# The first sample's mixed weight is spread over the quadrants by TensorE, and the first layer 0 moves up behind the mixtures

## The reference

```
x = x + (sum_k att0[b,k] W0[k]) @ x + att0 @ bias0        # conditional 1x1 layer
x = x + grouped_conv(x, 9 taps, 4 groups) + c_weight @ cond + fside
x = x + (sum_k att2[b,k] W2[k]) @ x + att2 @ bias2
x = x + (sum_k att3[b,k] W3[k]) @ x + att3 @ bias3
att_n = softmax(gelu(gelu(cond W0 + b0) W1 + b1) W2 + b2)   # K = 8 options
```

## Time and profile before

| | |
|---|---|
| median of 3 runs | 484.31 us (484.07 to 484.46) |
| the profiled execution | 484.36 us |
| its span, first to last instruction | 482.5 us |
| TensorE busy, of the span | 476.7 us (99%) |
| VectorE, ScalarE, GpSimd busy | 321.0, 249.0, 152.3 us |
| granted TensorE clock, mean | 1.00 |

### The profile page before, as it was taken

The page is one execution under the profiler, slowest core; times in us unless marked ns, Lnnn a source line. Parts: engine busy times, 40 slices in busy tenths (PEclk is TensorE's granted clock), DMA queues, the critical chain, the costliest instruction groups (busy, mean ns, idle before and its releaser), DMA issues.

```text
span 482.5 us, 17714 instructions
## 1 busy us (share of the span) xinstructions
PE 476.7 (99%) x8003; PEld 472.3 (98%) x8003; DVE 321.0 (67%) x409; ACT 249.0 (52%) x414; POOL 152.3 (32%) x151
## 2 busy tenths in 40 slices
PE   8999999999999999999999999999999999999996
PEld 8988999999999999999999999999999999999996
DVE  2648697767676876766687776767777676777424
ACT  3664455466444545654455466444545654455544
POOL 2935172324243222413331331434233142320110
PEclk9999999999999999999999999999999999999999
DMA  8696977676546477664657667464767746452224
GB/s 283 205 332 161 306 243 224 215 221 210 186 119 211 155 221 219 205 220 114 201 151 215 214 215 217 125 210 134 215 206 220 219 150 206 130 188 78 90 88 175
DMA packets 39243, 92.86 MB, mean 192 GB/s; under 512 B 4600, under 2 KB 25472, under 8 KB 35200
## 3 DMA queue, kind: packets, MB, share of 16 engines
q1 hardware_dynamic: 39168, 91.73, 61.2%
HBM read 53.95 MB, written 37.77 MB: 190 GB/s over the span
## 4 chain that ended last, share of the span: by engine, by line
PE 98%; DMA 0%; DVE 0%; issue 0%; DVEq 0%
PE cv_ps L499 56%; PE aux_ps L479 18%; PE aux_ps L528 17%; PE cv_ps L435 2%; PE cv_ps L422 1%; PE aux_ps L422 1%; PE cv_ps L528 1%; DMA m_rep<-in_net_dram 0%; PE aux_ps L457 0%; PE cv_ps L401 0%; PE aux_ps L376 0%; PE cv_ps L376 0%; DVE y_all L838 0%; PE aux_ps L391 0%; PE aux_ps L446 0%
## 5 line engine op out<-in xcount | busy, mean ns | idle before, releaser
L499 PE MATMUL cv_ps<-x_hi,conv_lo 32*128 32x512 f32 x1536 | 322.5, 391 | 0.0
L499 PE MATMUL cv_ps<-x_hi,conv_hi 32*128 32x512 f32 x1536 | 322.2, 389 | 0.0
L499 PE MATMUL cv_ps<-x_lo,conv_hi 32*128 32x512 f32 x1536 | 322.0, 391 | 0.0
L499 PEld LDWEIGHTS cv_ps<-x_hi,conv_lo 32*128 32x128 f32 x1536 | 202.6, 183 | 0.4
L499 PEld LDWEIGHTS cv_ps<-x_hi,conv_hi 32*128 32x128 f32 x1536 | 202.5, 183 | 0.4
L499 PEld LDWEIGHTS cv_ps<-x_lo,conv_hi 32*128 32x128 f32 x1536 | 202.4, 184 | 0.3
L770 DVE SCALAR_TENSOR_TENSOR x_lo<-cv_ps,d_all,x_hi 128x512 fp32r<-128x512 f32 x128 | 87.2, 743 | 131.0 <-ACT x_hi L617 131.0
L627 ACT ACTIVATE y_all<-aux_ps,e_all 128x512 f32<-128x512 f32 x122 | 74.0, 690 | 134.1 <-PE aux_ps L528 134.1
L479 PE MATMUL aux_ps<-x_hi,a_hi 32*128 32x512 f32 x512 | 115.5, 391 | 0.3 <-issue 0.3
L479 PE MATMUL aux_ps<-x_lo,a_hi 32*128 32x512 f32 x512 | 114.8, 388 | 0.0
L479 PE MATMUL aux_ps<-x_hi,a_lo 32*128 32x512 f32 x512 | 114.8, 388 | 0.0
(11 more groups left out here) (104 smaller groups left out, 512.4 us busy)
## 6 DMA issues: line engine op xcount, KB each, us to landing
x_sb<-in_x_dram SPq DMA_DIRECT2D x31, 1024.0 KB, 6.5
out_dram<-y_all SPq DMA_DIRECT2D x60, 512.0 KB, 7.4
a_rep<-a_pairs SPq DMA_DIRECT2D x64, 128.0 KB, 7.2
m_rep<-m_pairs SPq DMA_DIRECT2D x64, 128.0 KB, 6.3
out_dram<-y_all SPq DMA_DIRECT2D x8, 256.0 KB, 2.6
a_pairs<-a_all SPq DMA_DIRECT2D x1, 1920.0 KB, 11.3
m_pairs<-m_all SPq DMA_DIRECT2D x1, 1792.0 KB, 11.8
m_all<-in_mix_dram SPq DMA_DIRECT2D x2, 512.0 KB, 5.3
```

What stands on the lines that cost most here:

```text
L499: mm = pe.matmul(cv_ps[:, g, :], w[rows(g), j, :], a[n % 2][rows(g), q, s:s + T], start=(i == 0), stop=(i == steps - 1))
```

## The change

- The weight of sample 0 no longer goes through DRAM to its first use. Behind mixture 12+c quadrant c multiplies its 32 rows of `a0_all` by a 32 by 128 block of identities, which puts them on all 128 partitions of bank c of `cv_ps`. ScalarE makes the high part of the four results, VectorE the low part (`a0_first_hi`, `a0_split`). `split_a0(0)` of GpSimd goes.
- These four banks are slots 16 to 19 of the ring of 7, so mixture t has slot t up to 15 and slot t+4 from there on. The order of the banks in the ring is another one, and so is `BY_SCALAR`: 14 of 24 copies on ScalarE as before.
- Layer 0 of sample 0 follows in each quadrant directly behind its last mixture. Then comes the whole of the last bias, then all eight groups of pair products, then the steady part.
- The first biases stand behind turn 15 and not 11. The empty places of the first three turns take six idle matmuls.
- SP issues the load of the second x ahead of its first wait, and that of the third x ahead of the large save of `a0_all`.

```diff
-BY_SCALAR = [t % 2 == 0 or t in (9, 21) for t in range(MIXES)]
+BY_SCALAR = [t in (0, 2, 4, 6, 8, 9, 10, 12, 14, 16, 18, 19, 21, 22) for t in range(MIXES)]
+EARLY = 4 * LANES
...
-        mix_ps = [*prep_ps, aux_ps[:, 2, :], aux_ps[:, 3, :], aux_ps[:, 0, :]]
+        mix_ps = [aux_ps[:, 2, :], aux_ps[:, 3, :], *(cv_ps[:, g, :] for g in range(G)), aux_ps[:, 0, :]]
...
+        def mix_slot(t):
+            return t if t < EARLY else t + LANES
...
+        def slot_taken(slot):
+            if EARLY <= slot < EARLY + LANES:
+                return a0_split, 2
+            return mix_taken(slot if slot < EARLY else slot - LANES)
+        def l0_bank(n, p):
+            return cv_ps[:, 0, :] if n == 0 and p == PH - 1 else aux_ps[:, p + (n == 0), :]
...
@@ sync
             sp.dma_start(conv_f[:], conv).then_inc(conv_loaded, DMA)
+            load(1)
             sp.wait_ge(d_ready, 1)
...
             replicate_a0(0, range(PH))
-            load(1)
+            load(2)
             save(a0_all, a0_dram, 1, B // PAIR, a0_saved[1])
-            load(2)
@@ tensor, mixtures(c)
                 for _ in range(c):
+                    pe.matmul(mix_ps[c][:, 0:P], idle_sb[rows(c), 0:P].bitcast(F32),
+                              idle_sb[rows(c), P:2 * P].bitcast(F32), start=True, stop=True)
                     yield
...
-                        pe.wait_ge(*mix_taken(t - MIX_RING))
+                        pe.wait_ge(*slot_taken(mix_slot(t) - MIX_RING))
...
+                    if t + LANES in range(EARLY, EARLY + LANES):
+                        pe.wait_ge(*slot_taken(EARLY + c - MIX_RING))
+                        if c == 0:
+                            pe.wait_ge(*mix_taken(NOG - 2))
+                            pe.wait_ge(*mix_taken(NOG - 1))
+                        pe.matmul(cv_ps[:, c, 0:P], eyes_sb[rows(c)], a0_all[rows(c), 0, :], start=True,
+                                  stop=True).then_inc(a0_spread, 1)
+                        yield
@@ layer0_steps(n, p)
-                if n == 0 and p == 0:
-                    pe.wait_ge(e_out, 1)
-                pe.wait_ge(a0_split, 2 * (n + 1))
+                if p == 0:
+                    pe.wait_ge(a0_split, 2 * (n + 1))
+                if n == 0:
+                    if p == 0:
+                        pe.wait_ge(bias_out, 1)
+                        pe.wait_ge(c2_att_ready, 1)
+                    else:
+                        pe.wait_ge(*mix_taken(EARLY + p))
...
@@ the order on TensorE
-            mixing = [mixtures(c) for c in range(LANES)]
-            in_turn(mixing, 3 * G)
+            mixing = [itertools.chain(mixtures(c), layer0_steps(0, c)) for c in range(LANES)]
+            in_turn(mixing, EARLY)
             biases()
-            in_turn(mixing, 2 * G)
-            bias_e(range(0, 4))
             in_turn(mixing)
-            bias_e(range(4, K)).then_inc(e_made, 1)
-            for m in range(4):
-                quad_product(m)
-            in_turn([layer0_steps(0, p) for p in range(PH)])
-            for m in range(4, B // QUAD):
+            bias_e().then_inc(e_made, 1)
+            for m in range(B // QUAD):
                 quad_product(m)
@@ scalar
-            for t in range(MIXES):
+            for t in range(EARLY):
                 if BY_SCALAR[t]:
                     mix_evacuate(t)
-            for m in range(3):
-                m_evacuate(m)
+            act.wait_ge(a0_spread, LANES)
+            nc.scalar.activation(a0_hi[0][:], cv_ps[:, :, 0:P], ACT.Identity).then_inc(a0_first_hi, 1)
+            for t in range(EARLY, MIXES):
+                if BY_SCALAR[t]:
+                    mix_evacuate(t)
             split_second_x_hi(0)
-            m_evacuate(3)
-            split_second_x_hi(1)
             act.wait_ge(bias_out, 1)
             x1_out(0)
-            for m in range(4, B // QUAD):
+            split_second_x_hi(1)
+            for m in range(B // QUAD):
                 m_evacuate(m)
@@ vector, behind the copies of t < 16 and the small biases
+            dve.wait_ge(a0_first_hi, 1)
+            nc.vector.tensor_tensor(a0_lo[0][:], cv_ps[:, :, 0:P], a0_hi[0][:].bitcast(F32),
+                                    ALU.subtract).then_inc(a0_split, 2)
```

More of the change, by code:

```diff
@@ L218, in cond_resid_kernel @@
         conv_split = sem("conv_split")
+        a0_spread = sem("a0_spread")
+        a0_first_hi = sem("a0_first_hi")
         a0_split = sem("a0_split")
@@ L259, in cond_resid_kernel @@
         att_t_ps = aux_ps[0:K, 1, 0:NB].rearrange("k (n b) -> k n b", b=B)
-        c0_ps, d_ps, c2_ps, e_ps = (aux_ps[:, 1, P + B * i:P + B * (i + 1)] for i in range(4))
+        c0_ps, d_ps, c2_ps = (aux_ps[:, 1, P + B * i:P + B * (i + 1)] for i in range(3))
+        e_ps = aux_ps[:, 0, 0:B]
         att3_ps = aux_ps[:, 1, 2 * P:2 * P + K * B].rearrange("p (k n) -> p k n", k=K)
@@ L400, in fill @@
                 for _ in range(n):
-                    pe.matmul(prep_ps[1][:, 0:2 * P], idle_sb[:, 0:P], idle_sb[:], start=True, stop=True)
+                    pe.matmul(cv_ps[:, 3, 0:2 * P], idle_sb[:, 0:P], idle_sb[:], start=True, stop=True)
             def bias_d():
@@ L421, in mixtures @@
                     for j in range(G):
-                        mm = pe.matmul(mix_ps[t % MIX_RING][:, P * j:P * (j + 1)], mix_f[layer][rows(c), G * h + j, :],
+                        mm = pe.matmul(mix_ps[mix_slot(t) % MIX_RING][:, P * j:P * (j + 1)], mix_f[layer][rows(c), G * h + j, :],
                                        spread[rows(c), layer].rearrange("p b o -> p (b o)"), start=True, stop=True)
@@ L448, in biases, with bias_e @@
                 pe.matmul(c2_ps, bias_sb[:, 1, :], att_t[:, 1, :], start=True, stop=True).then_inc(c_made, 1)
-            def bias_e(options):
-                if 0 in options:
-                    pe.wait_ge(e_loaded, DMA)
-                    pe.wait_ge(c2_att_ready, 1)
-                    for n in range(1, NL):
-                        pe.matmul(e_ps, bias_sb[:, n, :], att_t[:, n, :], start=(n == 1), stop=False)
-                for k in options:
+            def bias_e():
+                pe.wait_ge(e_loaded, DMA)
+                pe.wait_ge(c2_att_ready, 1)
+                pe.wait_ge(*mix_taken(MIXES - 1))
+                for n in range(1, NL):
+                    pe.matmul(e_ps, bias_sb[:, n, :], att_t[:, n, :], start=(n == 1), stop=False)
+                for k in range(K):
                     mm = pe.matmul(e_ps, w3_sb[:, k, :], c2_att[:, k, :], start=False, stop=(k == K - 1))
@@ L462, in layer0_steps @@
             def layer0_steps(n, p):
-                if n == 0 and p == 0:
-                    pe.wait_ge(e_out, 1)
-                pe.wait_ge(a0_split, 2 * (n + 1))
-                wait(pe, y_out, PH * (n - 3) + p + 1)
-                if n in (1, 2):
-                    pe.wait_ge(x1_lo_done, PH * (n - 1) + p + 1)
+                if p == 0:
[3 more added lines that the diff above has]
+                        pe.wait_ge(bias_out, 1)
+                        pe.wait_ge(c2_att_ready, 1)
+                    else:
+                        pe.wait_ge(*mix_taken(EARLY + p))
+                elif n == 1:
+                    if p == 0:
+                        pe.wait_ge(e_out, 1)
+                    else:
+                        pe.wait_ge(x1_lo_done, p)
+                elif n == 2:
+                    pe.wait_ge(x1_lo_done, PH + p + 1)
+                else:
+                    pe.wait_ge(y_out, PH * (n - 3) + p + 1)
                 i, steps = 0, 3 * G
@@ L478, in layer0_steps @@
                     for w, a in ((a0_hi, hi), (a0_lo, hi), (a0_hi, lo)):
-                        mm = pe.matmul(aux_ps[:, p, :], w[n % 2][rows(p), g, :], a[rows(p), g % PER, :],
+                        mm = pe.matmul(l0_bank(n, p), w[n % 2][rows(p), g, :], a[rows(p), g % PER, :],
                                        start=(i == 0), stop=(i == steps - 1))
@@ L803, in _ @@
             nc.vector.tensor_scalar(d_sb[:], d_ps, fside_sb, None, ALU.add).then_inc(d_ready, 1)
-            for t in range(2 * LANES):
+            for t in range(EARLY):
                 if not BY_SCALAR[t]:
```

29 lines of the change are left out of this document (16 added, 13 removed).

## The result

| | before | changed |
|---|---|---|
| median | 484.38 us (484.07 to 485.4, 4 runs) | **489.31 us** (489.28 to 489.92, 4 runs) |
| ratio | | **1.0102**, 95% interval 1.0087 to 1.0118 |
| the profiled execution | 484.36 us | 489.33 us |
| its span | 482.5 us | 487.5 us |
| granted TensorE clock, mean | 1.00 | 0.993 |

The kernel became 4.9 us slower. The forecast was 488.0, with a range of 486.3 to 489.8, so the measured time lies in the range and 1.3 us above the forecast. It is not the likeliest case's time, but that of a rival, which the prediction had priced at 489.4.

The account below looks back on a forecast made before the run. TensorE, busy 476.7 of 482.5 us, was taken to bound the kernel. Its prologue terms put layer 0 of sample 1 at 37.5 instead of 33.84, +3.7 us on 484.36, giving 488.0, with a range of 486.3 to 489.8.

Parts of the forecast that it names:

- the likeliest case: Forecast itself: steady part starts 3.7 us later, all of it in turns 16 to 20; 488.0 us, chance 0.62.
- a rival: Clock falls in the waits of turns 16 to 20, 2.9 us at half pace lose 1.45; 489.4 us, chance 0.18.
- the chain of waits: Turns 16 to 20: four waits in a chain hold all quadrants, moving turn 20 from 16.85 to 22.53.
- turn 16: Turns 12 to 15 end at 16.18, the first biases take 0.67, so turn 16 starts at 16.85.
- turns 17, 18, 19: Mixtures 16 to 18 wait for copies 13, 14, 15, each just behind its matmul: +1.25, +1.20, +1.30 us.
- turn 20, behind the split: Mixture 19 waits for the fourth spread's high part on ScalarE, then low part on VectorE: 1.93 us, to 22.53.
- turns 20 to 27: Turns 20 to 23 at 0.22 each, then waits for copies; turn 28 starts at 24.8.
- layer 0's last turns and the last bias: Twelve turns of layer 0 take 2.8 us, to 27.6; the last bias, 1.27 and 1.01 in one piece, to 29.9.
- pair products: Eight groups ahead of layer 0 of sample 1 take 3.84 + 3.77 = 7.61 us, to 37.5.
- The last link: Turn 20 behind turn 19's fourth spread and its two-step split: 1.93 us, last of the four waits.
- What was costed at nothing: Six idle matmuls at 0; small biases on VectorE, GpSimd's split and the earlier x loads hidden.
- The gain of the change: Around layer 0 of sample 0: 0.30 wait before it, slow first two turns (0.73 against 0.46) and 0.30 behind it go.

Follow-up runs that it names:

- the one-piece order: Kernel before, only reordered: last bias and all pair products in one piece each, layer 0 of sample 0 opening the steady part, second x loaded early; 483.78 us, ratio 0.9991.
- The last two kernels: Kernel before with the order in one piece, no spread (483.78 us), and the same with banks in order and convolution waits one phase at a time (483.11 us).
- the last kernel: Order in one piece, with pair products and layer 0 taking banks in order and the convolution waiting one phase at a time; 483.11 us, ratio 0.998 to kernel before.

## Why the prediction was right, and where it was wrong

It was right in sign, in place and in its range. Of the 4.97 us the chain of waits, its own mechanism, is the larger part; what brought the time from its 488.0 to 489.3 is a cause that it had named and priced only as a rival. Point by point, with the start of the steady part as the sum, 37.5 predicted and 38.81 found:

| step | predicted | found | difference |
|---|---|---|---|
| turn 16 | 16.85 | 16.76 | -0.09 |
| turns 17, 18, 19 | +1.25, +1.20, +1.30 | +1.38, +1.22, +1.32 | +0.17 |
| turn 20, behind the split | +1.93 | +2.29 | +0.36 |
| turns 20 to 27 | 2.27 | 3.43 | +1.16 |
| layer 0's last turns and the last bias | 5.1 | 5.19 | +0.09 |
| pair products | 7.61 | 7.22 | -0.39 |
| sum | 37.5 | 38.81 | +1.3 |

- **The chain of waits**, the heart of the prediction, is there in each link, put down to VectorE, ScalarE, VectorE and VectorE as foretold. The three ring waits are 0.17 us off together. With the spreads behind the last mixtures the ring waits are gone, and with the clock at its full level in both records the steady part is 1.3 us sooner than with the real matmuls (35.99 against 37.31). So the ring waits were a cause and not only in the place of one, though that gain is net of the longer wait for the split, 1.81.
- **The step that failed is the clock.** The prediction kept 0.22 us per turn for turns 20 to 23 and had turn 28 at 24.8; it came at 26.40, at 0.43 per turn. It gave this rival 0.18 with 489.4. Its picture of the waits was even too dark: it had TensorE at work for 1 us out of 5.7, and the window 16.80:22.50 has it busy for 3.02, and still the clock fell. The real matmuls in the waits, which change nothing else in the order, take 1.5 us away and land at 487.84, beside the forecast's 488.0; that is what shows it. That both numbers fit so closely is in part luck. 489.4 was worked out from 2.9 us at half pace; the lower level lasted 6.8 us, of which 2.9 lie ahead of turn 20, more than half of them in waits that were there anyway. And at the full clock turns 20 to 27 take 1.93 and the pair products 7.22, 0.34 and 0.39 less than predicted, which makes up for a later turn 20 (23.21 against 22.53). Its reason for the low chance was that no row of before shows a fall. That is the absence of a case, not evidence: before, TensorE never waited so often in so short a time.
The Trainium skill, TensorE: Matmul & The Clock Gate, A second HAM failure mode, describes this pattern: short idle times between groups of matmuls that cycle through PSUM banks make the clock swing. The trace agrees as far as one fall goes, with 0.50 granted from 20.1 to 26.9 behind waits of 0.92, 0.54 and 0.62 us; it shows no second one. By that rule the forecast would have been the rival's 489.4.
- **The last link** took 0.36 more than its 1.93, for the most part by the same fall: its two passes ended 0.80 behind the start of turn 19 (20.68 to 21.48), where 0.43 was predicted. With the biases in the first wait the clock was still up at this place, and the link took 22.40 - 20.42 = 1.98. So the term of the forecast is sound, and the rest belongs to the clock's price.
- **Turns 0 to 15.** "Turns 0 to 11 are as before" was off twice, and the two nearly cancel. The mixtures began 0.34 later (10.22), behind constants that landed later; the prediction named no such cost, and the transfer of its own for the identities did not take it away. And the faster pace set in at 13.3 instead of 14.5, which made up for it. Together that is 0.09 at turn 16.
- **The pair products** take 7.23 in one piece, not 3.84 + 3.77. The prediction took over the length of two pieces for one. A piece of 32 products takes 3.84 in the kernel before (the row at 22.51 of the earlier trace rows); all 64 in the one-piece order, by TensorE's timeline:

```profile
22.02 7.39 PE L438 MATMUL cv_ps<-m_all,y_all 128*128 128x128 f32 x64
```

Two pieces of 3.84 are 0.29 longer than one of 7.39, so some 0.3 us of each piece are its start and its end and not its products (an estimate from these two lengths). The changed kernel and every variant in which nothing interrupts the piece have 7.23 in their chains. The idle time that the prediction saw between 29.70 and 30.00 was none: the last row of layer 0 in the earlier trace rows is busy until 29.47 + 0.60 = 30.07.
The Trainium skill, TensorEngine Tiling (Array Packing), Key Properties, says that a change of the tiling mode drains TensorE. The 0.38 less with one piece fewer agrees with it in sign; the page gives no figure. A drain ahead of the last bias, by which the sum would have been 0.3 more, cannot be seen, as that term is only 0.09 off.
The prediction counted two changes fewer between quadrants and whole array; by the order of the program it is four, since the first half of the last bias had interrupted the mixtures too.
- **What was costed at nothing** was nothing: the x loads, the small biases on VectorE and GpSimd's split, which ended at 25.66 + 1.28 = 26.94, long before 38.81. For the six idle matmuls it holds as well (1.0001).
- **The gain of the change.** The prediction put the idle time that the change removes at 0.9 and called it real. Of that only the 0.30 in front of layer 0 is idle in the trace, and the idle matmuls alone show what it is: the visible end of a gate at GpSimd's low part. The last two kernels hide that gate with no spread at all.

## What to carry to other kernels

When work goes into a ring of buffers, count how far the reuse of each buffer is from its last use, at the new place, for each following user: here four slots turned a distance of four turns into none, and because one in-order engine serves all four quadrants, every wait stopped all of them, at 1.22 to 1.38 us for each loop of matmul, copy and matmul. Then ask what the engine's clock does in the new gaps, and price it for all the work behind them: it gave back a repair of the gaps twice, once with the first biases moved into a wait and once, in good part, with the last bias moved into the last gap. And before making an operand sooner by extra work, look whether its first use can go later, behind work that needs nothing: that gave the only version whose interval lies below the kernel before, by 0.2%.

## What the runs showed of the hardware

- **A clock lost without a long gap.** In the changed kernel no idle stretch before the fall was over 0.92 us, and yet the granted clock went from 1.00 to 0.50 for 6.8 us. With the spreads behind all mixtures one gap of 1.81 us, with TensorE busy for 3.67 of the 4 us before 20, left it at 1.00 in the profiled execution, though perhaps not in the three others. So the length of the longest gap alone does not decide it; what does was not separated.
- **Busy is not enough.** With matmuls of zeros in the waits the columns read busy for all of 18 to 24 us and the clock fell as before; with real matmuls of 32 rows in the quadrants, which left 0.17 us of idle time in each of two waits, it did not. The two differ in data, in number and in shape, so which of these matters stays open. Under the last bias, 16 matmuls of 32 columns, it fell as well (0.71 at 23 to 24), with TensorE reading busy from 22 on, though busy for only 0.48 of the us from 19 to 20.
- **The clock column doesn't show the slow start.** It says 1.00 from 9 us to the rise and beyond it in every kernel, while the passes take 0.42 until the rise, as they do where the column reads 0.50, and 0.27 behind it. The rise came at about 12.7 us (the six idle matmuls alone), 13.1 (one piece), 13.3 (the changed kernel), 14.7 (before) and 19.6 (the last kernel), TensorE's program up to the end of the mixtures being the same in the second and the last of these. What sets it was not found.
